# A mixture-of-experts layer that adds each tile's result into token sums in DRAM, with weight conversions cut into pieces

## The chip, the core and the metric

The kernel runs on one core of one Trainium2 chip. The metric is device time in microseconds (us) of one execution, from the first to the last instruction with what lies around them. A median of three runs stands for the kernel; the profile is one further execution under the hardware profiler.

The core has a tensor engine (PE, with its weight loads shown as PEld), a vector engine (DVE), an activation engine (ACT), a general engine (POOL) and a sync engine (SP) that mostly issues transfers. Each runs its own instruction stream in order; they wait for each other by semaphores. A transfer (DMA) is issued by SP, ACT or POOL and raises a semaphore by 16 when it has landed.

## The reference, cut to what matters

One decoder layer on 8 x 112 tokens of width 256: self-attention, cross-attention with 375 context rows, and a feed-forward part with 8 experts of which each token uses the two with the largest gate value, plus one shared expert that all tokens use. Each part is followed by a residual addition and a layer norm. Only the last part is touched:

```
gate_out = x @ gate_w;  top_v, top_i = top_k(gate_out, 2)
probs = softmax over the two chosen;  w = probs where chosen, else 0
swiglu(x, w1, w2, w3) = (h * sigmoid(h) * (x @ w2)) @ w3,  h = x @ w1
out = sum over experts of swiglu(x, ew1[e], ew2[e], ew3[e]) * w[..., e]
out = out + swiglu(x, sw1, sw2, sw3)
x = layernorm(x + out)
```

An expert has w1 and w2 of 256 x 512 and w3 of 512 x 256. All arrays are float32.

## The kernel before

`decoder_layer` runs three blocks: preparation, attention (to 623 us of the profile) and `ffn_block`. The change lies in `ffn_block`, but for the few lines of the attention block that fill the DRAM buffer of the expert inputs.

Weights arrive as float32 and are used as pairs of float16 numbers (a `hi` part and the rest, `lo`), so that each product is three matmuls. There are nine weight sets: set 0 is the shared expert, set j is expert j-1. SP loads a set with three transfers of 512 KB each (`load_weights`, L382 and L384) into one of three raw buffers (`raw[j % 3]`). ACT writes the hi part, 1024 columns at a time (L1547), and DVE the lo part (L1616 from `convert`, tile w_ex). A set is therefore three such steps on either engine. A raw buffer is free for set j when DVE has converted set j-3 (`set_free`, semaphore w_lo).

**Head.** PE transposes the tokens (L1849) and computes the gate logits. DVE finds the top two (`top_two`), the row of the expert buffer that each (token, choice) pair goes to (`slots`), and the two weights (`top_weights`). POOL then writes 16 groups of 112 token rows to those places in the DRAM buffer moe_in with indirect DMAs (L1519). Meanwhile the shared expert is computed in eight units, (`unit`; four column blocks times two token halves; `silu` on ACT, `gate` on DVE, `unit_hi` and `unit_lo` for the pair) and eight output products `shared_down(b)`, which DVE adds to the residual in `ffn_res` (`shared_out`, L1753).

**Tile loop.** The expert buffer has 21 tiles of 128 rows, each of one expert; tiles 0 to 7 belong to experts 0 to 7, the others to experts read from a table. For each tile SP loads the rows (L1473, tile xs_in, four buffers), PE transposes them (L1935, ps_tok), ACT and DVE write the pair (`x_hi` L1565, `x_lo` L1616), PE makes the two products with w1 and w2 (`up`), ACT and DVE make the gated product (`silu` L1554, `gate` L1743), PE transposes it (L1927), ACT and DVE write its pair (`g_hi` L1571, `g_lo` L1762), PE multiplies by w3 (`down`, L1948), ACT copies the result out with a common scale (`y_copy`, L1577) and stores it to the DRAM buffer moe_out (`y_store`, L1581). PE runs the products of tile t+1 around the rest of tile t. In the tiles 0 to 5 ACT and DVE also convert weight set t+3 (`CONVERT`). PE waits before the products of tile t until set t+1 is converted (`up`: w_lo).

**End.** When all 21 results are stored, POOL gathers 16 groups of 112 rows (L1527, tile spare), two for each batch entry. DVE multiplies each by its weight and adds it to `ffn_res` (L1809), and takes mean and variance (L1812, L1814). POOL raises the variance to the power -0.5 (L1532), DVE and ACT normalise (L1827, L1610), SP stores the output in four transfers (L1487). In the profile, tiles that share memory have one name: y_sb and the gt pair appear as gsh_hi, the gathered rows as spare, the normalised output as store.

## Time and profile before

| | us |
|---|---|
| median of 3 runs | 853.75 (852.53 to 855.59) |
| the profiled execution | 857.23 |
| its span, first to last instruction | 855.4 |
| attention block ends, ffn block starts | about 623 |
| first tile transposed | 697.4 |
| first tile's result copied, by | 709.7 |
| the last two tiles' results copied, by | 818.94 and 822.24 |

The profile's page has busy times by engine, the chain that ended last, and groups of instructions by source line. A timeline row has the start, the duration, engine, line, operation and tiles, and in square brackets the idle time of that engine just before and what ended it. The tensor engine runs at one of two clock levels, 1.2 and 2.4 GHz; PEclk in a window is the mean as a share of 2.4 GHz, so 0.50 is the lower level all the time.

### The profile page before, as it was taken

The page shows a single profiled execution, that of the slowest core. Times are in us where ns is not written, and L with a number is a line of the kernel's source. Part 1 is how long each engine was busy: PE and PEld are TensorE (multiplying, and loading weights), DVE is VectorE, ACT ScalarE, POOL GpSimd, SP SyncE. Part 2 cuts the span into 40 slices and gives each one's busy share as a digit, 9 for nine tenths or more (in the row PEclk, how much of TensorE's full clock was granted, in tenths as well). Part 3 has the DMA queues.
Part 4 walks back from the last instruction along what each step waited for, and adds up shares of the span by engine and source line. Part 5 has one row for each costly group of instructions (what it writes and reads, how often), then busy time and mean ns, then how long its engine had stood idle before and what let it go on. Part 6 is the DMA issues. An engine that isn't in the chain of part 4 may idle for free. (4 is left out here: it accounts for less than half of the span.)

```text
span 855.4 us, 13435 instructions
## 1 busy us (share of the span) xinstructions
PE 667.5 (78%) x4168; PEld 534.3 (62%) x4168; DVE 547.2 (64%) x1137; ACT 411.5 (48%) x1021; POOL 196.7 (23%) x215
## 2 busy tenths in 40 slices
PE   5727589898899899899899899886767636789930
PEld 4516477777787788678678678675654523456620
DVE  3964357877867877886876886868465227633325
ACT  3313265575565574575574574554335116634411
POOL 3540031331331231231231231222126000000034
PEclk9855779999989989999989999999669869989975
DMA  8022201101100200200200200302164035311113
GB/s 286 31 81 72 60 1 29 56 25 35 50 25 13 70 25 11 72 25 11 72 25 11 72 25 11 123 26 76 48 221 142 19 110 173 117 39 61 39 52 95
DMA packets 54545, 54.18 MB, mean 63 GB/s; under 512 B 17448, under 2 KB 43376, under 8 KB 54512
## 3 DMA queue, kind: packets, MB, share of 16 engines
q1 hardware_dynamic: 49648, 46.73, 17.4%
q0 software_dynamic: 1840, 4.26, 1.7%
q10 hardware_dynamic: 3024, 2.75, 0.9%
q8 instruction: 19, 0.31, 0.2%
q14 instruction: 14, 0.11, 0.0%
HBM read 44.56 MB, written 9.18 MB: 63 GB/s over the span
## 5 line engine op out<-in xcount | busy, mean ns | idle before, releaser
L579 POOL TENSOR_TENSOR probs<-probs,c_rcp 112x750 f32<-112x750 f32 x64 | 92.0, 1437 | 319.1 <-DVE c_rcp L939 319.1
L702 ACT ACTIVATE probs<-ps_s,c_neg 112x375 f32<-112x375 f32 x128 | 72.3, 574 | 30.5 <-DVE c_neg L931 30.2
L1841 PE MATMUL ps_h<-w_ex,xst_hi 128*128 (+1 forms) x168 | 61.0, 406 | 16.8 <-issue 15.8
L1240 PE MATMUL ps_t<-ident,probs 112*125 112x112 f32 x384 | 56.3, 284 | 21.4 <-DVE cpt_lo L943 21.3
L1240 PEld LDWEIGHTS ps_t<-ident,probs 112*125 112x125 f32 x384 | 50.0, 195 | 29.0 <-issue 24.5
L929 DVE TENSOR_REDUCE c_max<-ps_s 112x2 f32<-112x750 f32 x64 | 59.8, 935 | 2.5 <-PE ps_s L131 1.6
L610 ACT ACTIVATE kt_hi<-ps_o 128x376 fp32r<-128x376 f32 x64 | 31.4, 491 | 58.9 <-PE ps_o L131 58.9
L129 PE MATMUL ps_o<-cpt_hi,v_lo 125*128 125x224 f32 x192 | 58.2, 303 | 2.0 <-DVE kt_lo L818 1.7
L943 DVE TENSOR_TENSOR cpt_lo<-ps_t,cpt_hi 125x672 fp32r<-125x672 f32 x64 | 54.6, 854 | 6.0 <-ACT cpt_hi L610 5.9
L129 PE MATMUL ps_o<-ctxt_hi,w_k_lo 128*128 128x376 f32 x128 | 50.1, 392 | 10.1 <-DVE oct_lo L818 10.0
L610 ACT ACTIVATE oct_hi<-ps_o 64x112 fp32r<-64x112 f32 x128 | 33.0, 258 | 49.3 <-PE ps_o L131 47.8
L130 PE MATMUL ps_o<-cpt_lo,v_hi 125*128 125x224 f32 x192 | 53.8, 280 | 0.0
L131 PE MATMUL ps_o<-cpt_hi,v_hi 125*128 125x224 f32 x192 | 53.7, 280 | 0.0
L1527 POOL DMA_INDIRECT spare<-moe_out,slot x16 | 14.9, 931 | 164.5 <-DMA moe_out<-gsh_hi 159.9
L1762 DVE TENSOR_TENSOR gsh_hi<-ps_g,gsh_hi 128x512 f16<-128x512 f32 x21 | 14.5, 692 | 57.3 <-ACT gsh_hi L1571 57.3
L610 ACT ACTIVATE v_hi<-ps_vx 125x512 fp32r<-125x512 f32 x48 | 28.7, 599 | 44.2 <-PE ps_vx L131 44.2
L818 DVE TENSOR_TENSOR oct_lo<-ps_o,oct_hi 64x112 fp32r<-64x112 f32 x128 | 34.7, 271 | 22.5 <-ACT oct_hi L610 20.4
L818 DVE TENSOR_TENSOR v_lo<-ps_vx,v_hi 125x512 fp32r<-125x512 f32 x48 | 32.9, 685 | 24.0 <-ACT v_hi L610 24.0
L610 ACT ACTIVATE cpt_hi<-ps_t 125x672 fp32r<-125x672 f32 x64 | 46.9, 733 | 1.4
L130 PE MATMUL ps_o<-ctxt_lo,w_k_hi 128*128 128x376 f32 x128 | 45.6, 356 | 0.0
L131 PE MATMUL ps_o<-ctxt_hi,w_k_hi 128*128 128x376 f32 x128 | 45.6, 356 | 0.0
L1554 ACT ACTIVATE s_act<-ps_h,unscale 128x512 f32<-128x512 f32 (+1 forms) x29 | 19.4, 670 | 53.1 <-PE ps_h L1841 48.2
(286 smaller groups left out, 1977.8 us busy)
## 6 DMA issues: line engine op xcount, KB each, us to landing
chunk<-in_L_ffn_ew_dram SPq DMA_DIRECT2D x24, 512.0 KB, 3.6
spare<-in_L_ffn_ew_dram SPq DMA_DIRECT2D x18, 512.0 KB, 6.2
store<-in_L_ffn_ew_dram SPq DMA_DIRECT2D x6, 512.0 KB, 5.3
ctx_raw<-in_ctx_dram SPq DMA_DIRECT2D x8, 375.0 KB
moe_in<-chunk SPq DMA_DIRECT2D x1, 2688.0 KB, 13.4
xs_in<-moe_in SPq DMA_DIRECT2D x21, 128.0 KB, 2.1
moe_out<-gsh_hi ACTq DMA_DIRECT2D x21, 128.0 KB, 1.7
plain_raw<-in_L_xattn_w_kv_dram SPq DMA_DIRECT2D x2, 1024.0 KB, 15.0
```

What stands on the lines that cost most here:

```text
L129: eng.matmul(out, ll, rh, start=start, stop=False, **kw)
L130: eng.matmul(out, lh, rl, start=False, stop=False, **kw)
L131: return eng.matmul(out, lh, rh, start=False, stop=stop, **kw)
L579: pool.tensor_tensor(p, p, r, ALU.mult).then_inc(sg["p_normed"], 1)
L610: return act.activation(dst, src, ACT.Copy)
L702: act.activation(probs[:, s % 2, h, :], ps_s[0:N, h, 0:SK], ACT.Exp, bias=c_neg[:, s % 2, h:h + 1], scale=CROSS_SCALE, accum_out=c_sum[:, ...
L818: return dve.tensor_tensor(dst, src, part.bitcast(F32), ALU.subtract)
L929: dve.reduce_max(c_max[:, s % 2, :], ps_s[0:N, :, 0:SK], X).then_inc(sg["c_max_ready"], 1)
L943: dve.tensor_tensor(cpt[1][:, :, :, :].rearrange("p h t n -> p h (t n)"), ps_t[0:SKT, :, 0:ST * N], cpt[0][:, :, :, :].rearrange("p h t n ...
L1240: last = pe.transpose(ps_t[0:SKT, h, t * N:(t + 1) * N], probs[:, s % 2, h, t * SKT:(t + 1) * SKT], ident[0:N, 0:N])
L1554: act.activation(s_act[:, u % 2, 0:cols], ps_h[:, 2 * (u % 2), 0:cols], ACT.Silu, scale=unscale[:, 0:1])\
L1841: last = pe.matmul(out, lhs[a], rhs[b], start=start and n == 0, stop=stop and n == 2)
```

## The change

Rows of the expert buffer become 258 numbers wide: the token's 256, its weight (with the result's common scale multiplied in) and its token number. DVE copies the tokens twice into such rows (`copy_rows`, in the memory of the last two experts' weights), POOL writes the token numbers, DVE the weights. Empty slots hold weight 0 and the number of an extra row after the tokens (`chunk` in the attention block, once, near 57 us). `y_copy` scales by the weight in the tile's own rows, which have six buffers instead of four.

The buffer moe_out, its 21 stores and the 16 gathers go. In their place is moe_sum in DRAM, a row for each token. SP first stores `ffn_res` there in two halves. POOL then adds each tile's result to the rows named in the tile with an indirect DMA that accumulates; two of them may name the same token, so each waits until the one before has landed (semaphore added). `y_copy(t)` waits for the addition of tile t-3, and the load of tile t for that of tile t-6. At the end SP reads the sums back in two transfers, and DVE takes the moments, without weighted additions.

Conversions are cut: single steps of the sets 1, 2 and 3 stand behind the units of the shared expert, and during tile t (0 to 4) set t+4 is converted, one step between `gate` and `g_lo`, two behind. Last, PE makes the transpose for the weight scales after the first four token transposes, not after all 16.

```diff
+XW = D + 2
+TB = 6
...
-        CONVERT = {t: [t + 3] for t in range(EXP - 2)}
+        HEAD_PIECES = [(j, i) for j in (1, 2, 3) for i in range(3)]
+        TILE_PIECES = {t: [(t + 4, i) for i in range(3)] for t in range(EXP - 3)}
...
             def load_tile(t):
-                if t >= 4:
-                    sp.wait_ge(sg["xt_full"], t - 3)
-                sp.dma_start(xs_in[:, t % 4, :], xs[t * P:(t + 1) * P, :]).then_inc(sg[f"xs_loaded{t % 4}"], 16)
+                if t >= TB:
+                    sp.wait_ge(sg["added"], 16 * (t - TB + 1))
+                sp.dma_start(xs_in[:, t % TB, :], xs[t * P:(t + 1) * P, :]).then_inc(sg[f"xs_loaded{t % TB}"], 16)
 
             for j in range(1, 6):
                 load_set(j)
+            for hf in range(2):
+                h = slice(4 * hf, 4 * hf + 4)
+                sp.wait_ge(sg["shared_out"], 4 * hf + 4)
+                sp.dma_start(acc[0:TOK, :].rearrange("(b n) d -> n b d", n=N)[:, h, :], res[:, h, :]).then_inc(sg["sums_started"], 16)
+            load_set(6)
             sp.wait_ge(sg["scattered"], 16 * 2 * B)
             for t in range(TILES):
-                if 6 <= t < 9:
-                    load_set(t)
+                if TB <= t < TB + 2:
+                    load_set(t - TB + 7)
                 load_tile(t)
+            for hf in range(2):
+                sp.wait_ge(sg["added"], 16 * TILES)
+                h = slice(4 * hf, 4 * hf + 4)
+                sp.dma_start(res[:, h, :], acc[0:TOK, :].rearrange("(b n) d -> n b d", n=N)[:, h, :]).then_inc(sg[f"summed{hf}"], 16)
...
-            for i in range(3):
-                pool.wait_ge(sg[f"y_stored{i}"], 16 * (TILES // 3))
-            for b in range(B):
-                for c in range(2):
-                    i = c * B + b
-                    pool.indirect_dma_start(gathered[:, 2 * b + c, :], None, ys[:, :],
-                                            bass.IndirectOffsetOnAxis(slot[:, i:i + 1], 0)).then_inc(sg[f"gathered{b // 2}"], 16)
+            pool.wait_ge(sg["sums_started"], 32)
+            for t in range(TILES):
+                pool.wait_ge(sg["y_ready"], t + 1)
+                if t >= 1:
+                    pool.wait_ge(sg["added"], 16 * t)
+                pool.indirect_dma_start(acc[:, :], bass.IndirectOffsetOnAxis(xs_in[:, t % TB, D + 1:D + 2].bitcast(U32), 0),
+                                        y_sb[:, t % 3, :], None, compute_op=ALU.add).then_inc(sg["added"], 16)
...
                 if t >= 3:
-                    act.wait_ge(sg[f"y_stored{t % 3}"], 16 * (t // 3))
-                act.activation(y_sb[:, t % 3, :], ps_y[:, 0:D], ACT.Copy, scale=c_y[:, 0:1]).then_inc(sg["y_ready"], 1)
...
+                    act.wait_ge(sg["added"], 16 * (t - 2))
+                act.activation(y_sb[:, t % 3, :], ps_y[:, 0:D], ACT.Copy, scale=xs_in[:, t % TB, D:D + 1]).then_inc(sg["y_ready"], 1)
...
+            def copy_rows():
+                for c in range(2):
+                    dve.tensor_copy(rows[:, c, :, 0:D], x2_all[0:N, :, :]).then_inc(sg["rows"], 1)
...
             for u in range(UNITS):
                 gate(u, HALF)
                 if u == 0:
+                    top_weights()
                     slots()
                 if u >= 1:
                     unit_lo(u - 1)
                 if u == 1:
                     over_tiles()
-                    top_weights()
-                if u == 3:
-                    convert(1)
+                if u >= 1:
+                    convert(*HEAD_PIECES[u - 1])
...
             for t in range(TILES):
                 gate(unit_of(t), 512)
+                pieces = TILE_PIECES.get(t, ())
+                for piece in pieces[0:1]:
+                    convert(*piece)
                 g_lo(t)
                 if t + 2 < TILES:
                     x_lo(t + 2)
-                for j in CONVERT.get(t, ()):
-                    convert(j)
...
+                for piece in pieces[1:]:
+                    convert(*piece)
...
+            def moments(b):
+                dve.wait_ge(sg[f"summed{b // 4}"], 16)
+                dve.bn_stats(stats[:, b, :], res[:, b, :]).then_inc(sg["y_stats"], 1)
```

On SP, from the loads of set 5 to the middle of the tile loads. Before:

```order
L382 DMA spare<-in_L_ffn_ew_dram 128x2x512 x2
L384 DMA spare<-in_L_ffn_ew_dram 128x4x256
L1473 DMA xs_in<-moe_in 128x256 x6
L382 DMA store<-in_L_ffn_ew_dram 128x2x512 x2
L384 DMA store<-in_L_ffn_ew_dram 128x4x256
L1473 DMA xs_in<-moe_in 128x256
```

and in the change:

```order
L384 DMA spare<-in_L_ffn_ew_dram 128x2x512 x2
L386 DMA spare<-in_L_ffn_ew_dram 128x4x256
L1484 DMA moe_sum<-ffn_res 112x4x256 x2
L384 DMA store<-in_L_ffn_ew_dram 128x2x512 x2
L386 DMA store<-in_L_ffn_ew_dram 128x4x256
L1477 DMA xs_in<-moe_in 128x258 x6
```

The two stores of the started sums and the load of set 6 now stand ahead of the first tile's load.

On DVE, the end of the head and the first tile with its conversion. Before (w_ex rows are lo steps of a set, ffn_res is `shared_out`, g is `gate`, gsh_hi from ps_g is `g_lo`):

```order
L1753 SCALAR_TENSOR_TENSOR ffn_res<-ps_g,c_y,x_all 112x256
L1616 SCALAR_TENSOR_TENSOR w_ex<-spare,s_cols,w_ex 128x1024 x3
L1616 SCALAR_TENSOR_TENSOR xst_lo<-ps_tok,xst_hi 128x256 x2
L1743 SCALAR_TENSOR_TENSOR g<-ps_h,c_gate,s_act 128x512
L1762 TENSOR_TENSOR gsh_hi<-ps_g,gsh_hi 128x512
L1616 SCALAR_TENSOR_TENSOR xst_lo<-ps_tok,xst_hi 128x256
L1616 SCALAR_TENSOR_TENSOR w_ex<-store,s_cols,w_ex 128x1024 x3
L1743 SCALAR_TENSOR_TENSOR g<-ps_h,c_gate,s_act 128x512
```

and in the change:

```order
L1630 SCALAR_TENSOR_TENSOR w_ex<-store,s_cols,w_ex 128x1024
L1772 SCALAR_TENSOR_TENSOR ffn_res<-ps_out,c_y,x_all 112x256
L1772 SCALAR_TENSOR_TENSOR ffn_res<-ps_g,c_y,x_all 112x256
L1630 SCALAR_TENSOR_TENSOR xst_lo<-ps_tok,xst_hi 128x256 x2
L1762 SCALAR_TENSOR_TENSOR g<-ps_h,c_gate,s_act 128x512
L1630 SCALAR_TENSOR_TENSOR w_ex<-spare,s_cols,w_ex 128x1024
L1781 TENSOR_TENSOR gsh_hi<-ps_g,gsh_hi 128x512
L1630 SCALAR_TENSOR_TENSOR xst_lo<-ps_tok,xst_hi 128x256
L1630 SCALAR_TENSOR_TENSOR w_ex<-spare,s_cols,w_ex 128x1024 x2
L1762 SCALAR_TENSOR_TENSOR g<-ps_h,c_gate,s_act 128x512
```

The lump of three steps behind the last `shared_out` is gone, and the steps during tile 0 are those of set 4 (before: set 3).

## Rows read from the trace of the kernel before

**Rows 1.** The page: busy time by engine.
```profile
PE 667.5 (78%) x4168; PEld 534.3 (62%) x4168; DVE 547.2 (64%) x1137; ACT 411.5 (48%) x1021; POOL 196.7 (23%) x215
```
**Rows 2.** Windows of ffn block: length, busy by engine, clock, DMA share, GB/s.
```profile
639.00:686.00 47.00, 33.37 (x199) 24.02 (x197) 20.47 (x47) 14.84 (x21) 16.31 (x17) 0.87 0.25 82
686.00:697.40 11.40, 0.00 (x0) 0.00 (x0) 3.45 (x3) 0.00 (x0) 0.00 (x0) 0.61 0.55 182
703.00:757.00 54.00, 38.20 (x202) 22.57 (x201) 34.18 (x40) 31.48 (x45) 0.00 (x0) 0.87 0.36 122
757.00:817.00 60.00, 59.95 (x390) 38.28 (x389) 21.30 (x38) 24.69 (x51) 0.00 (x0) 1.00 0.15 47
822.00:855.40 33.40, 0.00 (x0) 0.00 (x0) 14.24 (x40) 2.42 (x5) 17.12 (x18) 0.54 0.29 86
```
**Rows 3.** Timeline of the end, from the last tile's gate.
```profile
817.24 0.74 DVE L1743 SCALAR_TENSOR_TENSOR g<-ps_h,c_gate,s_act 128x512 f32<-128x512 f32 x1
...
821.77 0.47 ACT L1577 ACTIVATE gsh_hi<-ps_out,c_y 128x256 f32<-128x256 f32 x1 [1.77 <-PE ps_out L1948]
...
824.78 0.98 POOL L1527 DMA_INDIRECT spare<-moe_out,slot  x1 [159.88 <-DMA moe_out<-gsh_hi]
...
848.71 0.43 DVE L1812 BATCH_NORM_STATS2 ffn_stats<-ffn_res 112x6 f32<-112x256 f32 x1
...
849.39 0.17 DVE L1819 TENSOR_SCALAR ffn_var<-ffn_mv 112x4 f32<-112x4 f32 x1
```
**Rows 4.** DMA issues by line: size each, median us from issue to landing.
```profile
chunk<-in_L_ffn_ew_dram SPq DMA_DIRECT2D x24, 512.0 KB, 3.6
xs_in<-moe_in SPq DMA_DIRECT2D x21, 128.0 KB, 2.1
moe_out<-gsh_hi ACTq DMA_DIRECT2D x21, 128.0 KB, 1.7
spare<-moe_out,slot POOLq DMA_INDIRECT x16, 2.7
```
**Rows 5.** DVE timeline of the tile loop: a conversion period, its ends, the steady pace.
```profile
703.60 0.75 DVE L1743 SCALAR_TENSOR_TENSOR g<-ps_h,c_gate,s_act 128x512 f32<-128x512 f32 x1 [0.37 <-PE ps_h L1841]
...
723.34 3.68 DVE L1616 SCALAR_TENSOR_TENSOR w_ex<-spare,s_cols,w_ex 128x1024 f16<-128x1024 f32 x3 [0.29 <-ACT w_ex L1547]
...
729.82 0.69 DVE L1762 TENSOR_TENSOR gsh_hi<-ps_g,gsh_hi 128x512 f16<-128x512 f32 x1 [2.14 <-ACT gsh_hi L1571]
730.42 0.41 DVE L1616 SCALAR_TENSOR_TENSOR xst_lo<-ps_tok,xst_hi 128x256 f16<-128x256 f32 x1
731.12 3.68 DVE L1616 SCALAR_TENSOR_TENSOR w_ex<-store,s_cols,w_ex 128x1024 f16<-128x1024 f32 x3 [0.29 <-ACT w_ex L1547]
...
757.17 0.75 DVE L1743 SCALAR_TENSOR_TENSOR g<-ps_h,c_gate,s_act 128x512 f32<-128x512 f32 x1 [1.13 <-issue]
```
**Rows 6.** The same period on PE and ACT.
```profile
727.12 0.38 PE L1841 MATMUL ps_h<-w_ex,xst_hi 128*128 128x512 f16 x1 [3.07 <-issue]
...
729.94 3.23 ACT L1547 ACTIVATE w_ex<-store,s_cols 128x1024 f16<-128x1024 f32 x3
```
**Rows 7.** Timeline of the head: what the shifts rest on.
```profile
627.36 0.16 DVE L1639 COPY p_cols<-ps_g 128x4 f32<-128x4 f32 x1 [2.43 <-PE ps_g L1852]
...
640.01 0.69 DVE L1743 SCALAR_TENSOR_TENSOR g<-ps_h,c_gate,s_act 128x448 f32<-128x448 f32 x1 [1.65 <-PE ps_h L1841]
...
657.34 0.32 PE L1841 MATMUL ps_out<-w_sh_hi,gsh_hi 128*112 128x256 f16 x1 [3.46 <-DVE gsh_lo L1748]
...
667.22 0.63 ACT L1554 ACTIVATE s_act<-ps_h,unscale 128x448 f32<-128x448 f32 x1 [4.89 <-remote]
...
685.78 3.67 DVE L1616 SCALAR_TENSOR_TENSOR w_ex<-spare,s_cols,w_ex 128x1024 f16<-128x1024 f32 x3
...
690.91 11.64 SPq L1473 DMA_DIRECT2D xs_in<-moe_in  x6
```
**Rows 8.** Line 908, a DVE cast within SBUF: min/median/max ns, first and last start.
```profile
L908 DVE CAST xnt_hi<-xnt_f x8: 277/1055/1142, 99.4 to 547.1; 128x224 fp32r<-128x224 f32 x8
```

104 lines of the change are left out of this document (53 added, 51 removed).

## The prediction

> **What bounds the kernel now.** I read the page first. PE is busy 78% of the span [rows 1], which would make it the engine to watch. But the change touches only the last 230 us, so I took that stretch in windows [rows 2]. The reader is to see five stages in them. In the head (639 to 686) PE is busy 33.4 of 47.0 us. From 686 to 697.4 it does nothing, while transfers run at a share of 0.55. In the first seven tiles (703 to 757) it is busy 38.2 of 54.0. From 757 to 817 it is busy 59.95 of 60.0 at full clock; there nothing but PE counts. From 822 on it is idle, and the 33.4 us go to POOL (17.1) and DVE (14.2). So PE is the bound in one stage of five, the one that the change leaves alone.
>
> The timeline names the waits. At the end [rows 3] the last result is copied at 821.77 and is out at 822.24. The first gather starts at 824.78. Sixteen gathers follow, 1.23 us apart, and the variance of the second half is ready at 849.56. In the tile loop [rows 5, 6] PE starts the products of the next tile at 727.12, after 3.07 us of idleness, right when DVE has ended the three conversion steps that began at 723.34 (3.68 us). Then the ring closes: products and transposition, the hi part on ACT, `g_lo` at 729.82, `x_lo` at 730.42, the next conversion at 731.12. One turn takes 7.78 us (723.34 to 731.12), and it is a ring of dependences, since set t+3 is converted during tile t and needed at once. Without conversions a tile takes 4.62 us: 13 tiles between the gates at 757.17 and 817.24 [rows 3, 5].
>
> **The end.** Before, from 822.24 to the span's end at 855.4, it takes 33.2 us. The change leaves this: the last addition waits for the one before it, is issued, and lands; two loads of 448 KB; four moments; variance, power, normalisation, stores.
> The round of one addition (wait seen, descriptors made, rows read, added, written, semaphore) has no row. The nearest is the gather, an indirect transfer by POOL of almost the same size: 2.7 us to landing [rows 4]. That is the low end. The high end takes fetching the sums, bringing the new rows and storing as three transfers one behind the other: 2.7 + 2.1 + 1.7 = 6.5 us [rows 4]. I take 3.9, nearer to the gather: 128 rows in place of 112 adds 0.1 to it, one read of DRAM inside the transfer a share of the 2.1, say 1.1.
> The last result comes 3.3 us after the one before (822.24 and 818.94 in the table of times), so the last addition starts 0.1 to 0.6 us late; it lands about 4.3 us after the copy. A load of 512 KB lands in 3.6 us [rows 4], so the first half of the sums is there after 3.4, the second 1.8 later. DVE needs for a half four moments of 0.43, four aggregations and the variance (0.25 lie between the last moments' end, 849.14, and the variance, so 0.5 for four in a row, and 0.2) [rows 3], 2.4 us in all; the second half's variance is ready 3.4 + 2.4 + 2.4 = 8.2 us after the landing, the second load being hidden behind the first half's moments. From there to the end of the span I keep the 6.0 us of before (849.4 to 855.4). Together 4.3 + 8.2 + 6.0 = 18.5, a gain of 14.7 us. At the ends of the round's range it is 15.9 and 12.1.
> The Trainium skill (DMA: Bandwidth & Descriptors, Anatomy of one DMA) gives a transfer issued by POOL a fixed cost of about 2.0 us, most of it the write receipt, plus its bytes over 436 GB/s. By that 128 KB take 2.3 us, an estimate, and with the making of the descriptors a round of 3.2 us, which would add 0.7 to the gain; the page has no figure for an accumulating transfer.
>
> **The tile loop.** Gate 0 to gate 7 took 757.17 - 703.60 = 53.6 us [rows 5]. Now five tiles carry conversions, and they are needed two tiles later, so the ring above is open. What is left is each engine's own work: DVE was busy 34.2 us in seven tiles with six conversions of 3.68, so 1.7 a tile without and 5.4 with one; ACT 31.5 with six of 3.23, so 1.7 and 5.0 [rows 2, 5, 6]. The two are coupled. From one `silu` ACT passes a step, the hi parts and two more steps, about 5 us; DVE's last step (1.2) and the next gate (0.7) follow: 6.9. From that gate PE transposes and makes three sets of products, nearly its whole tile of 4.62, before the `silu` after the next can start: 4.7. That is two tiles in 11.6 us, 5.8 each. So 5 x 5.8 + 2 x 4.62 + about 1 for the change of pace = 39.2, a gain of 14. Ends: at DVE's bare 5.4, 16.4; if a tile with conversions kept 7.78, only the sixth one is saved, 5.4.
> The store's issue on ACT (21 times) costs nothing before and brings nothing: ACT waits for PE in this stage. The two queues which the new waits stand in: `y_copy(t)` on ACT waits for addition t-3, behind it is the `silu` of the next tile; SP's load of tile t waits for addition t-6, behind it are later tile loads and set 8. Both have two tiles or more of room if a round is shorter than a tile. If it isn't, they pass the delay on; that is the first rival below.
>
> **The head.** The first tile is transposed at 697.4, when its rows have come. Its load is issued at 690.91, behind the load of set 5, which waited for DVE's lump of 3.67 us behind the last `shared_out` [rows 7]. Part by part:
> - The scale transpose moved ahead: p_cols came at 627.36 after 2.43 us of waiting. DVE can then do the tokens' lo parts as ACT delivers the hi parts; the gate product starts about 1.8 earlier. Gain 1.8.
> - Two copies of 112 x 2048 numbers on DVE before the first gate. A DVE step over 1024 numbers takes 1.23 us (3.68 for three) [rows 5], so 2.3 for 2048; at twice the pace 1.2 each. DVE was idle for 1.65 us there [rows 7], so the gate comes 0.8 to 3.0 later; say 2.35. With `top_weights` (0.85) now ahead of `slots` I book 3.2 as the loss. The scatter ends a few us later and is still ahead of SP's wait.
> - The lumps: PE's wait of 3.46 us for a `gsh_lo` behind a conversion shrinks by about 2; the lump behind the last `shared_out` goes, 3.7; steps now standing between `shared_out` 4 and 6 cost 1.2.
> - 448 KB more ahead of the first tile's rows. From 686 to 697.4 transfers moved 182 GB/s at a share of 0.55 [rows 2], so 330 with all engines busy: 1.4 us.
> - ACT stood still for 4.89 us at 667.22 with no releaser in the trace [rows 7]. I don't know its cause; with other orders and transfers it may go or stay: half, 2.4.
> Sum 1.8 - 3.2 + 2.0 + 3.7 - 1.2 - 1.4 + 2.4 = 4.1; I take 4. Ends: 10 (stall gone, its cold clock too, cheap copies) and -3 (stall stays, dear copies).
> One row bears on the copies: a DVE cast from SBUF to SBUF takes 277 ns at best, 1055 in the median [rows 8], in an attention stage where POOL runs multiplications. The Trainium skill (SBUF — State Buffer, on the shared port pair) says that a float32 copy within SBUF takes both ports of the pair and that whichever of DVE and POOL comes second stands still until the other has finished. By that rule the copies, which come while POOL raises the gaps to a power, would begin late by what is left of it, at most the 1.65 us that DVE had free, so the head would gain about 3 in place of 4, an estimate; and no DVE instruction of the tile loop is of that kind, so POOL's descriptors aren't starved there. The trace agrees as far as that cast shows.
> The wider rows, the first fill of the buffer with 0.1 us more on POOL near 57 us, and 1032-byte rows cost nothing: the fill is hidden behind attention.
>
> **Sum.** 14.7 + 14 + 4 = 32.7 us. The profiled execution took 857.2 (span 855.4 and 1.8 around it), so 824.5; the median of the runs is 3.5 below it: 821.
>
> **Rivals.**
> - Additions set the pace, still faster. They follow each other one round apart from the first result on, at about 705.7 (before 709.7, less the head's 4). 21 rounds plus 14.2 us to the end are later than the forecast once a round exceeds 4.9 us. For: each must land before the next, and DRAM is read and written. Against: the gather's 2.7. At 5.5 us: 705.7 + 115.5 + 14.2 = 835.4, less 1.7 for the runs' median: 834.
> - The same mechanism beyond 6.45 us a round makes the kernel slower: 21 x 6.5 gives 705.7 + 136.5 + 14.2 - 1.7 = 854.7. PE would stand waiting in each tile, its clock might drop. For: the 6.5 of three transfers in a row. Against: a single transfer's engines overlap the parts.
> - Conversions stay the pace: the pieces run, but `g_hi` and `g_lo` get stuck behind steps and a tile keeps 7.8 us, or set 7 or 8 comes late since SP waits for an addition ahead of it. Loop gain 5.4: 830. For: DVE is nearly full at 5.4. Against: two tiles of room.
> - The head goes wrong (first tile's rows late behind set 6 and the sums): head -3, 828.
>
> **Chances.** Forecast 0.64, with a range of its own of 812 to 830 (it takes in the last rival's size); additions as pace but faster 0.13; slower 0.06; conversions 0.12; head 0.05. A measurement here can tell about 0.3% from no change. Faster by more than that 0.91, within it 0.03, slower 0.06. The range for all is 809 to 842: the low end has the best of the head and loop (10 + 16.4 + 15.9 = 42.3, so 811, and 2 for the spread of the runs), the high end a round of 5.9 us.
>
> **What would show it.** The gap between additions in the loop equals the tile's pace (4.6), and from issue to landing is under 4.9. If the first term is right, last copy to span's end is 18 to 19 us. If the second is, gates 0 to 5 are 5.6 to 6 apart and PE's wait of 3.07 is gone. For the third, the first transpose stands 3 to 5 us earlier relative to the block's start; the stall without a releaser is there or not. The forecast is wrong if POOL's additions follow each other without a gap from the first tile on, or if PE is below full clock after the conversions.

## The result, and the profile after

The kernel after the change takes 821.5 us (median of four runs, 819.5 to 823.1), the kernel before 853.1 (851.1 to 855.6) beside it: a ratio of 0.963, with a 95% interval of 0.959 to 0.966. The forecast was 821. The profiled execution after took 820.8 us with a span of 819.0, against 857.2 and 855.4.

The page's busy times hardly move, except POOL's, which now issues 21 transfers that add (columns as in [rows 1] and in the page's costliest groups):

```profile
PE 658.7 (80%) x4168; PEld 527.8 (64%) x4168; DVE 540.1 (66%) x1124; ACT 411.2 (50%) x1021; POOL 218.4 (27%) x223
...
L1543 POOL DMA_INDIRECT moe_sum<-gsh_hi,xs_in x21 | 33.6, 1602 | 106.4 <-DMA moe_sum<-gsh_hi,xs_in 63.6
```

The last number is the one to see: of the time that POOL waits ahead of an addition, 63.6 us end with the landing of the addition before (36.6 more are the wait for the first result, and the rest, put down to others, are landings too: those results had been ready for 3 us). The forecast had POOL waiting for results.

The windows of the ffn block after, cut near the events of the table below (columns as in [rows 2]):

```profile
620.00:635.35 15.35, 13.58 (x97) 10.32 (x98) 12.89 (x51) 7.40 (x10) 4.27 (x16) 0.56 0.90 302
635.35:675.73 40.38, 30.09 (x179) 21.12 (x177) 27.43 (x54) 17.83 (x24) 18.44 (x16) 0.92 0.44 138
675.73:686.61 10.88, 0.66 (x2) 0.29 (x2) 0.00 (x0) 0.00 (x1) 0.00 (x0) 0.61 0.80 259
692.68:731.73 39.05, 32.15 (x202) 19.73 (x201) 29.81 (x36) 28.49 (x42) 10.48 (x6) 1.00 0.44 115
731.73:796.76 65.03, 63.26 (x414) 40.53 (x412) 22.95 (x41) 26.19 (x54) 20.08 (x13) 1.00 0.34 50
796.76:819.00 22.24, 0.00 (x0) 0.00 (x0) 5.13 (x24) 2.19 (x5) 5.30 (x4) 0.60 0.39 94
```

The first seven tiles take 39.05 us where they took 53.6 [rows 5]; the third window is a hole of 10.9 us in which the engines do almost nothing, with transfers at a share of 0.80; the last one is the end, 22.2 us where it was 33.2.

The end in the timeline, against [rows 3] (start, duration, engine, line, tiles, idle time and its releaser):

```profile
796.29 0.47 ACT L1594 ACTIVATE gsh_hi<-ps_out,xs_in 128x256 f32<-128x256 f32 x1 [1.76 <-DMA moe_sum<-gsh_hi,xs_in]
797.12 1.54 POOL L1543 DMA_INDIRECT moe_sum<-gsh_hi,xs_in  x1 [2.89 <-ACT gsh_hi L1594]
801.52 1.54 POOL L1543 DMA_INDIRECT moe_sum<-gsh_hi,xs_in  x1 [2.85 <-DMA moe_sum<-gsh_hi,xs_in]
805.16 0.86 SPq L1494 DMA_DIRECT2D ffn_res<-moe_sum  x2
809.46 1.40 DVE L1830 BATCH_NORM_STATS2 ffn_stats<-ffn_res 112x6 f32<-112x256 f32 x4 [14.21 <-DMA ffn_res<-moe_sum]
...
811.18 0.17 DVE L1839 TENSOR_SCALAR ffn_var<-ffn_mv 112x4 f32<-112x4 f32 x1
...
812.97 0.17 DVE L1839 TENSOR_SCALAR ffn_var<-ffn_mv 112x4 f32<-112x4 f32 x1
...
813.88 2.23 SPq L1500 DMA_DIRECT2D out_dram<-store  x4
```

The last result is copied by 796.76. At 797.12 POOL issues the addition of the tile *before*, whose result had been ready for 3.2 us (the profile names the last copy as what ended that wait, but the addition needs only its own); the last tile's follows at 801.52, 4.8 us after its copy, and has landed by 805.16, when SP reads the sums. From there the chain runs as foreseen: the second variance is ready 8.0 us later, and 5.9 us remain.

The list of DMA issues, against [rows 4] (size each, median us from issue to landing):

```profile
moe_sum<-ffn_res SPq DMA_DIRECT2D x2, 448.0 KB, 3.3
ffn_res<-moe_sum SPq DMA_DIRECT2D x2, 448.0 KB, 4.8
moe_sum<-gsh_hi,xs_in POOLq DMA_INDIRECT x21, 3.8
```

The chain of additions on POOL (same columns as the timeline), from the first on:

```profile
699.61 2.16 POOL L1543 DMA_INDIRECT moe_sum<-gsh_hi,xs_in  x1 [36.60 <-ACT gsh_hi L1594]
708.32 1.96 POOL L1543 DMA_INDIRECT moe_sum<-gsh_hi,xs_in  x1 [6.55 <-DMA moe_sum<-gsh_hi,xs_in]
716.48 1.74 POOL L1543 DMA_INDIRECT moe_sum<-gsh_hi,xs_in  x1 [6.21 <-DMA moe_sum<-gsh_hi,xs_in]
...
730.11 1.54 POOL L1543 DMA_INDIRECT moe_sum<-gsh_hi,xs_in  x1 [2.87 <-DMA moe_sum<-gsh_hi,xs_in]
734.61 1.54 POOL L1543 DMA_INDIRECT moe_sum<-gsh_hi,xs_in  x1 [2.95 <-DMA moe_sum<-gsh_hi,xs_in]
...
753.22 1.54 POOL L1543 DMA_INDIRECT moe_sum<-gsh_hi,xs_in  x1 [2.85 <-DMA moe_sum<-gsh_hi,xs_in]
759.82 1.54 POOL L1543 DMA_INDIRECT moe_sum<-gsh_hi,xs_in  x1 [5.06 <-DMA moe_sum<-gsh_hi,xs_in]
```

A usual round is about 4.5 us from start to start (4.4 to 4.8). The first two take 8.7 and 8.2: they run beside the loads of sets 7 and 8 (issued at 700.3 and 708.0). Three later ones take 5.3 to 6.6.

The tile loop on DVE, against [rows 5]: gate 0, the steps of tile 0, gate 7.

```profile
692.68 0.75 DVE L1762 SCALAR_TENSOR_TENSOR g<-ps_h,c_gate,s_act 128x512 f32<-128x512 f32 x1 [0.98 <-PE ps_h L1863]
695.67 1.29 DVE L1630 SCALAR_TENSOR_TENSOR w_ex<-spare,s_cols,w_ex 128x1024 f16<-128x1024 f32 x1 [2.23 <-ACT w_ex L1564]
696.87 0.68 DVE L1781 TENSOR_TENSOR gsh_hi<-ps_g,gsh_hi 128x512 f16<-128x512 f32 x1
697.47 0.42 DVE L1630 SCALAR_TENSOR_TENSOR xst_lo<-ps_tok,xst_hi 128x256 f16<-128x256 f32 x1
697.80 2.47 DVE L1630 SCALAR_TENSOR_TENSOR w_ex<-spare,s_cols,w_ex 128x1024 f16<-128x1024 f32 x2
...
731.73 0.74 DVE L1762 SCALAR_TENSOR_TENSOR g<-ps_h,c_gate,s_act 128x512 f32<-128x512 f32 x1
```

In the same stretch PE's 3.07 us of idleness in each tile [rows 6] are gone; what is left is a wait for the gate:

```profile
718.71 0.66 PE L1951 MATMUL ps_g<-ident,g 128*128 128x128 f32 x4 [1.06 <-DVE g L1762]
```

The head, against [rows 7]: p_cols, the copies, the first gate, and POOL's power beside them; then the first tile's transposition.

```profile
621.75 0.16 DVE L1656 COPY p_cols<-ps_g 128x4 f32<-128x4 f32 x1 [0.36 <-PE ps_g L1875]
...
632.52 1.82 POOL L1528 TENSOR_TENSOR gap_e<-euler,gap 112x8 f32<-112x8 f32 x1 [9.88 <-DVE gap L1685]
...
633.08 2.35 DVE L1639 COPY w_ex<-x_all 112x2048 f32<-112x2048 f32 x2
635.35 0.68 DVE L1762 SCALAR_TENSOR_TENSOR g<-ps_h,c_gate,s_act 128x448 f32<-128x448 f32 x1
...
685.91 0.66 PE L1959 MATMUL ps_tok<-ident,xs_in 128*128 128x128 f32 x2 [10.70 <-DMA xs_in<-moe_in]
```

p_cols waits 0.36 us and not 2.43. Both copies together take 2.35. And PE stands 10.7 us for the first tile's rows, whose load SP issued at 678.5, behind two stores that wait for `shared_out` and behind set 6.

**Where the time went, by stage.** One profiled execution of each kernel, all times counted from the first DVE instruction of the ffn block (623.6 before, 620.0 after), so that what lies ahead of the block drops out. Rows end at the start of the instruction that they name. The columns "again" and the two halves are experiments below.

| us | before | before again | pieces only | additions only | after | after again |
|---|---|---|---|---|---|---|
| block start to last `shared_out` | 61.8 | 57.3 | 55.0 | 54.6 | 55.2 | 55.2 |
| to `x_lo` of tile 0 | 13.2 | 12.3 | 7.4 | 15.8 | 11.8 | 11.6 |
| to gate 0 | 5.1 | 6.0 | 6.1 | 5.6 | 5.7 | 5.7 |
| gate 0 to gate 7 | 53.6 | 50.9 | 39.1 | 52.1 | 39.1 | 39.1 |
| gate 7 to the last copy's end | 65.1 | 65.1 | 64.9 | 64.6 | 65.0 | 64.6 |
| last copy's end to the span's end | 33.2 | 33.3 | 33.3 | 19.5 | 22.2 | 21.6 |
| sum | 231.8 | 224.7 | 205.8 | 212.1 | 199.0 | 197.7 |

Blocks began between 619.6 and 624.0 in the fourteen traces of this study with no relation to the kernel. That part is noise: 3.5 of the 36.4 us between the two spans.

### The profile page after: what moved, and what is told of

It reads as the page before. It is cut to its first block and busy times, and to the rows that moved or that the text cites. A ratio compares the mean times of both kernels' runs of the same rounds, so it can differ in the third digit from the quotient of the medians.

```text
span 819.0 us, 13429 instructions
## 1 busy us (share of the span) xinstructions
PE 658.7 (80%) x4168; PEld 527.8 (64%) x4168; DVE 540.1 (66%) x1124; ACT 411.2 (50%) x1021; POOL 218.4 (27%) x223
## 5 line engine op out<-in xcount | busy, mean ns | idle before, releaser
L1543 POOL DMA_INDIRECT moe_sum<-gsh_hi,xs_in x21 | 33.6, 1602 | 106.4 <-DMA moe_sum<-gsh_hi,xs_in 63.6
L1863 PE MATMUL ps_h<-w_ex,xst_hi 128*128 (+1 forms) x168 | 58.2, 389 | 1.4 <-DVE xst_lo L1630 0.9
L946 DVE TENSOR_TENSOR cpt_lo<-ps_t,cpt_hi 125x672 fp32r<-125x672 f32 x64 | 54.6, 853 | 6.0 <-ACT cpt_hi L613 5.9
L1781 DVE TENSOR_TENSOR gsh_hi<-ps_g,gsh_hi 128x512 f16<-128x512 f32 x21 | 14.5, 690 | 45.0 <-ACT gsh_hi L1588 45.0
L639 ACT ACTIVATE work<-ps_a,s_neg 112x112 f32<-112x112 f32 x128 | 35.1, 379 | 16.5 <-DVE s_neg L851 16.4
```

The costliest lines, as they stand in the source:

```text
L639: last = act.activation(e_self[:, 4 * f + j, :], bank(f"S{f}")[0:N, j * N:(j + 1) * N], ACT.Exp, bias=s_neg[:, f, j:j + 1], scale=SELF_SCALE)
L946: dve.tensor_tensor(cpt[1][:, :, :, :].rearrange("p h t n -> p h (t n)"), ps_t[0:SKT, :, 0:ST * N], cpt[0][:, :, :, :].rearrange("p h t n ...
L1863: last = pe.matmul(out, lhs[a], rhs[b], start=start and n == 0, stop=stop and n == 2)
```

## The experiments

Each kernel changes the one named, and was timed beside the kernel before. Ratios are to that kernel; it ran at 847.8, 848.7 and 847.8 us in the three comparisons, not at 853.

**The two halves apart.** First the conversions alone, in the kernel before:

```diff
-        CONVERT = {t: [t + 3] for t in range(EXP - 2)}
+        HEAD_PIECES = [(j, i) for j in (1, 2, 3) for i in range(3)]
+        TILE_PIECES = {t: [(t + 4, i) for i in range(3)] for t in range(EXP - 3)}
...
-            for j in range(1, 6):
+            for j in range(1, 7):
                 load_set(j)
```

> The kernel before with one part of the change: weight conversions in pieces, a set earlier, and set 6 loaded ahead of the tiles. The results are stored and gathered as before. If the terms of my sum add up, this keeps the loop's gain (14.5 us as the trace after shows it) and the part of the head's gain that comes from the lumps (about 5 of 8): ratio 0.977, some 833 us; gate 0 to gate 7 about 39.5 us, last copy to the end of the span 33 us as before. Rival: the loop got faster only because ACT no longer issues a store in each tile and SP waits for other things; then gate 0 to gate 7 stays above 45 us and the time above 840.

Measured: 829.2 us, ratio 0.979 (0.975 to 0.982), gate 0 to gate 7 39.1, the end 33.3. Stores and gathers had no part in the loop's pace. The time is 4 us under what I had expected, since the kernel before ran at 848 here and not at 853; the ratio is the expected one.

The other half is the kernel after with the reverse edit:

```diff
-        HEAD_PIECES = [(j, i) for j in (1, 2, 3) for i in range(3)]
-        TILE_PIECES = {t: [(t + 4, i) for i in range(3)] for t in range(EXP - 3)}
+        CONVERT = {t: [t + 3] for t in range(EXP - 2)}
...
-            load_set(6)
...
-                if TB <= t < TB + 2:
-                    load_set(t - TB + 7)
+                if 6 <= t < 9:
+                    load_set(t)
```

> The changed kernel with the conversions put back into lumps of three steps at their old places (set t+3 behind tile t, SP's load of set 6 behind the tiles). If the terms add up, the loop takes 53.6 us from gate 0 to gate 7 as before, and the end keeps what the trace after shows or a little more: at 7.8 us a tile the additions fall no further behind, so the last one starts under 4 us after the last copy, and last copy to the end of the span is 21 to 22 us. With the cheaper head (no 4.9 us stall of ACT, copies 1.2 us each) about 3 more: 853 - 11.5 - 3 = 839 us, ratio 0.983. Rival: additions in flight slow the weight loads and the loop grows beyond 55 us: 842 or more.

Measured: 837.7 us, ratio 0.987 (0.983 to 0.991); the loop 52.1, the end 19.5, which is lower than I had it: at this pace the additions catch up completely, and the last one starts 2.0 us after the last copy. So the whole worth of the additions at the end is 13.8 us, close to the 14.7 of the forecast; the kernel after gets 11 to 11.7 of it.

**The two kernels once more,** unedited, for a second trace of each.

> The kernel before, unchanged, once more with a profile. In its first trace ACT stands still for 4.89 us at unit 6 of the shared expert, 4.3 of them after PE had ended what it waits for; no trace with any part of the change shows that. If the stall belongs to the kernel's program, it is here again at the same silu, with 4 to 5 us. If it belongs to that one execution, silu 6 follows the end of the conversion within 0.5 us of PE's products, the last shared_out is 4 to 5 us nearer to the start of the block (57 us after it in place of 61.8), and the span is about 850.

The stall was that one execution's. Here silu 6 follows the conversion at once (ACT, start and duration; compare the 4.89 in [rows 7]):

```profile
657.62 3.21 ACT L1547 ACTIVATE w_ex<-spare,s_cols 128x1024 f16<-128x1024 f32 x3
661.50 0.63 ACT L1554 ACTIVATE s_act<-ps_h,unscale 128x448 f32<-128x448 f32 x1 [0.68 <-PE ps_h L1841]
```

The execution took 848.6 us, and the last `shared_out` comes 57.3 us after the block's start. The loop too is 2.7 us shorter than in the first trace. I had worked the gains out of an execution that was 8.6 us slower than this one. Of the 24 runs of the kernel before in these three comparisons, 18 lie between 846.2 and 850.0 and six between 851.3 and 852.9; the four of the first comparison lie between 851.1 and 855.6. Nothing here tells why.

> The changed kernel, unchanged, on this chip beside the kernel before. With the two halves measured apart (0.9785 for the pieces, 0.9873 for the additions) their sum is 0.9658, against 0.9627 measured for both together on another chip. If the parts add up, this comes out between 0.962 and 0.966. Block-relative points of the trace as in the first one within 0.5 us: last shared_out 55.2, gate 0 to gate 7 39.1, last copy to the end of the span 22.2, and the additions 7, 10 and 16 again longer than 5 us.

Measured: 820.5 us, ratio 0.967 (0.963 to 0.971). Every stage repeats within 0.7 us. The halves' ratios (0.979 and 0.987) add up to 0.966. Their traces add up less well: beside before again the halves save 18.9 and 12.6 us inside the block, together 31.5, and the whole 27.0. Of the 4.5 that are missing, 2.1 lie at the end and 3.5 ahead of tile 0 (each half brings the last `shared_out` 2.3 to 2.7 us forward, both together 2.1); the loop gives 1.2 back. So the two parts are not quite independent. Long rounds came again, one of them at a tile where the first trace had one: 10 (5.1) and 13 (5.8).

**Is the length of a round the bound?** Between an addition's landing and the next one's issue, one more POOL operation:

```diff
                 if t >= 1:
                     pool.wait_ge(sg["added"], 16 * t)
+                    pool.tensor_tensor(held[:, :], euler[:, 0:4], neg_half[:, 0:4], ALU.pow).then_inc(sg["held"], 1)
+                    pool.wait_ge(sg["held"], t)
```

> The changed kernel with one more POOL operation, a power over 112x4 numbers (1.1 us in the trace after), between the landing of an addition and the issue of the next; it computes nothing that is used. A round grows from 4.43 to about 5.6 us and is longer than PE's tile of 4.66. If the chain of additions takes over at that point, the last 18 rounds take 18 x 5.6 from about 719 us: the last starts 18 us later and the time is 838 to 841 us. Rival: additions have slack as I predicted (two buffers and more) and only the end grows, by 1.2 to 5 us: 823 to 827.

Two rounds on POOL (columns as above; `held` is laid over `ffn_shift`):

```profile
736.86 1.04 POOL L1544 TENSOR_TENSOR ffn_shift<-euler,ffn_neg_half 112x4 f32<-112x4 f32 x1 [2.37 <-DMA moe_sum<-gsh_hi,xs_in]
738.19 1.60 POOL L1546 DMA_INDIRECT moe_sum<-gsh_hi,xs_in  x1 [0.29 <-POOL ffn_shift L1544]
742.07 1.04 POOL L1544 TENSOR_TENSOR ffn_shift<-euler,ffn_neg_half 112x4 f32<-112x4 f32 x1 [2.29 <-ACT gsh_hi L1597]
743.40 1.59 POOL L1546 DMA_INDIRECT moe_sum<-gsh_hi,xs_in  x1 [0.29 <-POOL ffn_shift L1544]
```

Measured: 835.0 us, ratio 0.986 (0.982 to 0.989). A round is 5.3 us (5.2 to 5.5), not 5.6, and the additions fall behind from tile to tile; the last starts 11.4 us after the last copy, and the end takes 29.0. Only at tiles 18 and 19 do the gates stretch (5.3 and 6.3 us), when `y_copy` finds no free buffer. The time lies between the two that I had named. So a bound is there, and by 5.3 us a round it has been passed; but the three result buffers let the delay pile up at the end instead of in the tiles.

**What in a round costs?** The same scatter without the adding:

```diff
-                                        y_sb[:, t % 3, :], None, compute_op=ALU.add).then_inc(sg["added"], 16)
+                                        y_sb[:, t % 3, :], None).then_inc(sg["added"], 16)
```

> The changed kernel with the scatter of each result writing its rows and not adding them (the sum of shared part and both experts is left out of the output); same indices, same waits. If adding is what makes a round 4.43 us long, a plain write's is 3.3 to 3.6, POOL's own part about 0.95 as in the other scatter, every write waits for its copy and the end is 18.7 us: 3 us less than the kernel after, ratio 0.960 against 0.9635. If it is the transfer's fixed cost with 128 rows, the round stays within 0.2 of 4.43 and the time is the same as after's.

The last two writes on POOL, and the trace's row of DMA issues:

```profile
795.27 0.96 POOL L1543 DMA_INDIRECT moe_sum<-gsh_hi,xs_in  x1 [3.46 <-ACT gsh_hi L1594]
798.41 0.96 POOL L1543 DMA_INDIRECT moe_sum<-gsh_hi,xs_in  x1 [2.18 <-ACT gsh_hi L1594]
```

```profile
moe_sum<-gsh_hi,xs_in POOLq DMA_INDIRECT x21, 2.4
```

Measured: 816.2 us, ratio 0.961 (0.957 to 0.964). This kernel leaves the sums out of its output. Adding makes POOL's part 1.54 us and not 0.96, and the landing 3.8 us after the issue and not 2.4: 1.4 us a round. Without it every write but the last waits for its result; the last waits for the landing, and its round of 3.14 us (795.27 to 798.41) is what a chain of plain writes would take. It starts 0.6 us after the copy and the end is 16.7 us, 2 less than I expected.

**Is waiting for one another the cost at the end?** Two accumulators, on top of the kernel with the tiles first (next paragraph): odd tiles add to a second one, which starts at zero.

```diff
+        def wait_added(eng, t):
+            eng.wait_ge(sg[f"added{t % 2}"], 16 * (t // 2 + 1))
...
-                if t >= 1:
-                    pool.wait_ge(sg["added"], 16 * t)
-                pool.indirect_dma_start(acc[:, :], bass.IndirectOffsetOnAxis(xs_in[:, t % TB, D + 1:D + 2].bitcast(U32), 0),
+                if t >= 2:
+                    wait_added(pool, t - 2)
+                pool.indirect_dma_start((acc, acc1)[t % 2][:, :], bass.IndirectOffsetOnAxis(xs_in[:, t % TB, D + 1:D + 2].bitcast(U32), 0),
...
+                dve.tensor_tensor(res[:, h, :], res[:, h, :], odd[:, h, :], ALU.add).then_inc(sg["y_stats"], 1)
```

> The kernel with the tiles' loads first, and with two accumulators in DRAM: even tiles add to one (started with the sums), odd tiles to the other (started with zeros from a store behind set 5's load). An addition waits only for the one two before it, so POOL always waits for the result instead. The odd sums are loaded while the last addition is on its way, and two DVE additions of 112x1024 numbers (about 1.1 us each) join the halves. If the 22.2 us of the end come from the chain (last addition 4.8 us late), the last addition starts within 0.6 us of the copy and lands some 4.4 us after it, 3.9 earlier than in the kernel after; the two joins give 2.3 back: last copy to the end 20.5 us, time 1.5 to 2 us under the kernel with the tiles first alone (ratio about 0.949). Rival: two additions in flight slow each other on the same queue, and the landing comes no earlier than 6.5 us after the issue: no gain or a loss of 1 to 2 us.

The last addition, the read of the even sums and the first join, from the timeline:

```profile
785.20 1.54 POOL L1559 DMA_INDIRECT moe_sum<-gsh_hi,xs_in  x1 [1.26 <-ACT gsh_hi L1611]
...
790.62 0.84 SPq L1509 DMA_DIRECT2D ffn_res<-moe_sum  x2
794.82 1.23 DVE L1849 TENSOR_TENSOR ffn_res<-ffn_res,spare 112x1024 f32<-112x1024 f32 x1 [11.41 <-DMA ffn_res<-moe_sum]
```

Measured: 808.7 us, ratio 0.951 (0.948 to 0.955), the same as with one accumulator; the end 22.0 us in both. All additions but the first (0.78) start 0.27 us after their copies, as said. But SP reads the sums 5.4 us after the last issue, where it is 3.6 in the kernel after: another addition, issued 2.8 us before, and the loads of the odd sums run beside it (which of them costs the 1.8 us was not taken apart). And the two joins take 2.46 us. What was saved in waiting is spent there.

**The first tile's rows.** SP's order alone: the six tile loads ahead of the stores of the sums and of set 6.

```diff
-            for hf in range(2):
-                h = slice(4 * hf, 4 * hf + 4)
-                sp.wait_ge(sg["shared_out"], 4 * hf + 4)
...
-            load_set(6)
             sp.wait_ge(sg["scattered"], 16 * 2 * B)
             for t in range(TILES):
+                if t == TB:
+                    for hf in range(2):
+                        h = slice(4 * hf, 4 * hf + 4)
+                        sp.wait_ge(sg["shared_out"], 4 * hf + 4)
...
+                    load_set(6)
                 if TB <= t < TB + 2:
```

> The changed kernel with one reordering on SP: the loads of the first six tiles' rows stand ahead of the two stores of the started sums and of set 6's load. In the trace after, PE waits 10.7 us for the first tile's rows behind set 6's 1.5 MB. If the queue's order is the cause, the first tile is transposed some 9 us earlier against the start of the block and the time falls by 8 to 9.5 us, to about 812.5. Rival: set 6 then comes late, and tile 2's conversion waits for it: the gain is under 4 us. Second rival: the rows were not what PE needed next (x_lo on DVE behind the last shared_out): gain under 2.

Measured: 806.7 us, ratio 0.951 (0.948 to 0.954). That is 13.8 us under the kernel after where I had expected 8 to 9.5. `x_lo` of tile 0 stands 55.7 us after the block's start where it was 67.0, and gate 0, behind it, comes 3.6 us later and not 5.7: 13.4 us in all. PE goes from the shared expert to the first tile's transposition without a pause. The next kernel moves set 6 only:

```diff
-            load_set(6)
             sp.wait_ge(sg["scattered"], 16 * 2 * B)
             for t in range(TILES):
+                if t == TB:
+                    load_set(6)
                 if TB <= t < TB + 2:
```

> The changed kernel with only set 6's load moved behind the loads of the first six tiles; the stores of the started sums stay ahead. Of the 11.6 us that the first tile came earlier with the tiles first, this keeps what 1.5 MB in front of the rows cost and leaves what SP's waits for shared_out cost. The tile loads are then issued at about 56.2 us after the block's start, and land 3 us later behind 448 KB: x_lo of tile 0 at 59.5 to 60.5 (67.0 after, 55.7 with the tiles first); 6.5 us less than after, ratio about 0.959. Rival: SP's waits were the cause, the load of set 6 is cut short by nothing: x_lo 0 at 64 or later, ratio above 0.963.

Measured: 815.6 us, ratio 0.963 (0.959 to 0.966); `x_lo` at 59.3 us. Of the 11.3 us, 7.7 are set 6 in front of the rows (1.5 MB, and 2.3 us of SP's time to issue it), 3.6 the two stores with SP's waits for `shared_out`. The gain in time is smaller than the 7.7, about 5 us beside after's 820.5, and this trace ends with the last addition 5.4 us late.

**Lead or splitting?** The kernel after with three steps in one lump behind `x_hi` and `x_lo`, but still of the set needed two tiles later.

```diff
-                pieces = TILE_PIECES.get(t, ())
-                for piece in pieces[0:1]:
-                    convert(*piece)
                 g_lo(t)
                 if t + 2 < TILES:
                     x_lo(t + 2)
-                for piece in pieces[1:]:
+                for piece in TILE_PIECES.get(t, ()):
                     convert(*piece)
```

> The changed kernel with the three steps of a tile in one lump behind x_hi and x_lo, as before the change, but still of the set that is needed two tiles later. It tells what the lead does from what the splitting does. By my rings: the next gate stands behind DVE's lump, and ACT's next lump behind that gate's transposition: ACT's lump to DVE's end 4.3, gate 0.7, transposition 0.8, g_hi and x_hi 0.9, so 6.7 to 7 us a tile; gate 0 to gate 7 then takes 43 to 45 us (39.05 in the kernel after, 50.85 to 53.6 before), and the time is 4 to 5 us over the kernel after, ratio about 0.972. Rival: the lead is all of it, tiles stay at 5.9 and the time is after's (0.967). Second rival: splitting is all of it, 7.8 us a tile and 50.9 in all, ratio 0.980.

One turn on DVE, gate to gate:

```profile
708.09 0.75 DVE L1759 SCALAR_TENSOR_TENSOR g<-ps_h,c_gate,s_act 128x512 f32<-128x512 f32 x1
...
711.52 3.67 DVE L1627 SCALAR_TENSOR_TENSOR w_ex<-store,s_cols,w_ex 128x1024 f16<-128x1024 f32 x3 [0.29 <-ACT w_ex L1564]
715.12 0.74 DVE L1759 SCALAR_TENSOR_TENSOR g<-ps_h,c_gate,s_act 128x512 f32<-128x512 f32 x1
```

Measured: 823.6 us, ratio 0.971 (0.967 to 0.974). A tile takes 7.03 us and the loop 44.9. Of the 11.8 us that the loop gains over the second trace of before, the lead with one tile fewer gives 6.0, the splitting 5.8. The time rose by 3 and not by 5.8, since slower tiles let the additions catch up: the end is 19.6.

**One more set in the head.** On top of tiles first; set 4 is converted before the tiles.

```diff
-        HEAD_PIECES = [(j, i) for j in (1, 2, 3) for i in range(3)]
-        TILE_PIECES = {t: [(t + 4, i) for i in range(3)] for t in range(EXP - 3)}
+        HEAD_PIECES = [(j, i) for j in (1, 2, 3, 4) for i in range(3)]
+        ACT_AT = {6: (6, 7, 8), 7: (9, 10, 11)}
+        TILE_PIECES = {t: [(t + 5, i) for i in range(3)] for t in range(EXP - 4)}
...
-                if TB <= t < TB + 2:
-                    load_set(t - TB + 7)
+                    for j in (6, 7, 8):
+                        load_set(j)
```

> The kernel with the tiles' loads first, and with set 4 converted in the head too: steps of set 3 lie in the 6.5 us in which DVE and ACT wait for unit 7 of the shared expert, those of set 4 between the last shared_outs; four tiles in the loop carry conversions instead of five, and sets 6 to 8 are loaded ahead of tile 6's rows. If DVE's wait hides three steps, the last shared_out stays at 55 us after the block's start, gate 0 to gate 7 takes 1.25 us less (37.9), the first additions don't meet two set loads in a row, and the time is 1 to 2.5 us under the kernel with the tiles first. Rival: DVE ends its steps after unit 7 is ready, shared_out 2 comes late, PE waits: last shared_out over 57 us and no gain.

> The kernel with the loads of the first six tiles ahead of the stores and of set 6's load, once more and in more rounds, as the measure for the one before it on the same chip: ratio to the kernel before 0.951 as in its first run, last copy to the end 22.0 us with the last addition again 4.0 to 4.8 us behind the last copy.

Measured, with six and five executions: 804.9 us, ratio 0.947 (0.944 to 0.950), beside 808.8, 0.952 (0.950 to 0.955), for tiles first. The last `shared_out` at 54.6 us and the loop of 37.7 are as expected (1.5 us less). The time fell by 3.9, more than the 1 to 2.5 expected. The end brought more, 19.4 in place of 22.3 us. POOL's last two additions, first with four sets ahead:

```profile
781.30 1.54 POOL L1544 DMA_INDIRECT moe_sum<-gsh_hi,xs_in  x1 [2.92 <-ACT gsh_hi L1595]
785.84 1.54 POOL L1544 DMA_INDIRECT moe_sum<-gsh_hi,xs_in  x1 [2.99 <-DMA moe_sum<-gsh_hi,xs_in]
```

and with the tiles first only:

```profile
785.41 1.54 POOL L1544 DMA_INDIRECT moe_sum<-gsh_hi,xs_in  x1 [2.93 <-ACT gsh_hi L1595]
789.95 1.54 POOL L1544 DMA_INDIRECT moe_sum<-gsh_hi,xs_in  x1 [2.99 <-DMA moe_sum<-gsh_hi,xs_in]
```

The last copies end at 783.76 and 785.33: the last addition starts 2.1 and 4.6 us later. The table of delays shows when the chain fell behind, from a copy's end to its addition's start:

| tile | 1 | 2 | 3 | 5 | 8 | 11 | 14 | 17 | 19 | 20 |
|---|---|---|---|---|---|---|---|---|---|---|
| after | 3.3 | 5.7 | 4.1 | 1.4 | 1.9 | 3.1 | 2.6 | 3.4 | 3.2 | 4.8 |
| lumps, early | 2.5 | 3.3 | 0.3 | 0.3 | 0.3 | 0.3 | 0.3 | 0.3 | 0.3 | 2.0 |
| tiles first again | 3.3 | 5.7 | 4.2 | 1.3 | 2.0 | 2.5 | 3.1 | 3.1 | 2.9 | 4.6 |
| four sets ahead | 2.4 | 1.1 | 0.3 | 0.3 | 0.3 | 0.3 | 0.3 | 0.3 | 0.3 | 2.1 |

Where the first two additions don't meet two set loads, or the tiles are slow at first, the chain is in step by tile 3 and stays so; from tile 6 on no round of these kernels is over 5 us. In the kernels where it isn't in step by tile 5 it never is: an ordinary round takes 4.5 us, a tile 4.6 to 4.7, and with the odd longer round the mean round in after, from 716.48 to 801.52, is 4.72 us. The last column is 2 us even in step, since the last copy ends only 2.8 us after the one before (3.3 in the kernel before).

The longer rounds have a companion in the traces. The page counts a queue that carries instructions:

```profile
q8 instruction: 19, 0.31, 0.2%
```

These are packets of 16 KB that take 0.9 to 1.8 us each; in the tile loop one comes every three tiles or so. The five traces that never get in step (after twice, tiles first twice, set 6 behind) have 15 rounds of over 5 us from tile 3 on, all of them at the tiles 7, 10, 13 and 16, and in every one such a packet begins 1.9 to 3.9 us after the addition's issue. In ten other rounds it begins earlier, and they take 4.4 to 4.9 us. In the kernels in step the packets come at the same tiles from 7 on, but 3.2 to 4.5 us after the issue, and the additions land after 3.6 to 3.9 us as ever. So a chain that is in step has the packets behind its additions, and one that is late has them beside. That is a coincidence in time and not a cause shown: no kernel moves the packets, and three of the fifteen (3.3 to 3.9) begin at points that did no harm in step.

The best kernel is this last one, 16 us faster than the change as it was made.

## Why the prediction was right, and where it was not

The time was hit within half a microsecond. In the first pair of traces the block got 32.8 us shorter, where 32.7 were forecast, but not by the terms that I gave: the loop 14.5 (14 forecast), the end 11.0 (14.7), the head up to gate 0 7.4 (4). The second pair, without ACT's stall of 4.9 us, has 11.8, 11.7 and 3.0, and 0.5 between gate 7 and the last copy, 27.0 in all.

**The loop: right.** 39.2 us were forecast from coupling ACT's and DVE's work over two tiles; 39.05 came, with two tiles in 11.9 (11.6 forecast); the seven gates are 7.5, 5.8, 6.1, 5.8, 6.1, 3.1 and 4.7 us apart. The early lumps confirm the same way of counting (43 to 45 forecast, 44.9). The gain of 14 was too large in general, though. It rests on 53.6 us before, and 50.9 is what the second trace of before shows.

**The end: mis-sized, by 3.7 us.** The step that failed is "so the last addition starts 0.1 to 0.6 us late; it lands about 4.3 us after the copy". It starts 4.8 late, and the sums are read 8.4 after the copy. Of the 4.8, 2.0 come even in a chain that is in step: a round is 4.5 us and not 3.9, and the last copy comes 2.8 us after the one before and not 3.3. The other 2.7 are backlog: the first two rounds, beside set loads, are twice as long, and longer rounds in between eat the 0.1 to 0.2 us of slack of a tile. Once issued, the last addition is a little quicker than I had it, 3.6 us to the reading of the sums.

The working has an error besides. The round enters the sum twice, as the wait for the addition before and as the landing, and the ends that I gave (15.9 and 12.1) count its range once. With 6.5 us in both places the last addition starts 3.2 us late and lands 9.7 after the copy, a gain of 9.3; the measured 11.0 lies outside the ends as stated and inside these. The round itself lay inside the bounds (2.7 and 6.5), but I drew only "faster than 4.9: hidden" from them, and not what a chain with 2 to 3% of slack does after a disturbance. In step, as in the additions alone, the end is 19.5 us; my own sum gives 19.9 with 4.5 in both places. Everything behind the landing was right: 8.2 and 6.0 forecast, 8.0 and 5.9 measured.

The Trainium skill (DMA: Bandwidth & Descriptors, Anatomy of one DMA) led to 3.2 us by its fixed cost of about 2.0 us. The plain write agrees: 2.4 us from issue to landing beside the 2.3 worked out from the page, an estimate, and a round of 3.14. It does not hold for a transfer that adds, which lands 1.4 us later, and the measurement decides.

**The head: right sign, wrong terms.** Forecast 4, and 8.0 in the first pair up to the first transposition (73.9 to 65.9). But 4.9 of these are ACT's stall, which I had booked at half and which is no property of the kernel; the second pair shows 2.7 (69.6 to 66.8, up to `x_lo`). Moving the scale transposition gave 2.2 us at p_cols (1.8 forecast). The copies take 1.2 us each, my low price: the first gate came 1.1 us earlier, not 0.5 later. For copies and `top_weights` together I took 3.2; the last `shared_out` stands at 55.2 with them and with the 2.2 us gained, and at 55.0 in the pieces only, which have neither, so they cost 2.4. The load of set 6 and the waits ahead of the first rows, which I had booked at 1.4 us for bytes alone, cost up to 11.3. It is the largest thing that I missed: I priced a store and not set 6, 1.5 MB that stand in the same line. The stores were too cheap as well: I counted 448 KB, and both halves, 896 KB, stand ahead of the rows. In the additions only, where set 6 does not, `x_lo` of tile 0 comes 15.8 us behind the last `shared_out` and not 12.3; moving set 6 away leaves 3.6.

The copies also speak to the rule of the Trainium skill (SBUF — State Buffer, on the shared port pair) that the second of DVE and POOL stands still. They began at 633.08, in the middle of POOL's power (632.52 to 634.34), and took 1.17 us each; the power took 1.82 us where it took 1.68 before. No standstill shows; where page and measurement differ, the measurement decides. The forecast had weighed about 3 by the rule against 4 without.

**The base: too high, and luck.** I took the gain off a profiled execution and 3.5 us more, in effect off 853.7. The kernel before runs at 848 in three later comparisons, and the profile that I read was 8.6 above that. In the terms of two ordinary executions the change is worth 27 us inside the block (224.7 to 197.7), where I had 32.7. A base 5 to 6 us too high and a gain 5.7 too large cancel; that the forecast of 821 meets 821.5, and 820.5 the second time, is luck in this.

**The rivals.** "Additions set the pace" (0.13) is real: `held` has passed its point at 5.3 us a round, and the change itself, with a mean of 4.72, stands at it and pays 2.1 to 2.7 us. My own sign of being wrong, additions that follow each other without a gap from the first tile on, is there: from tile 1 on every addition starts 1.1 us or more behind its copy, where 0.27 is the least, and waits for the landing before it. The forecast of the time held all the same, because the buffers let the delay show only at the end. "Conversions stay the pace" is refuted by gates 5.83 and 6.06 apart. "The head goes wrong" was half true: the rows were late behind set 6, as its text says, but less late than before.

## What to carry to other kernels

- A chain of transfers that must wait for each other needs its round compared with the consumer's pace by the mean, disturbances included. At an ordinary 4.5 against 4.6 to 4.7 us a backlog of 5.7 us sank to 1.1 by tile 10, never went away and grew again; once in step the same chain stayed in step.
- When a load queue is in order, read what stands ahead of the *first* transfer that the next stage needs, its waits as well as its bytes. That one reordering was worth 12 to 14 us here, nearly half as much as the whole change.
- Profile the kernel before twice ahead of putting numbers on a difference. One stall of 4.9 us without a releaser stood in one trace and in none of the other thirteen, and with it half of the head's gain in the first pair.
